# Normalised rows and third parts on GpSimd in the distance stage of a hybrid layer

## The reference, cut to what matters

```python
xn = layernorm(x)                               # per row, eps 1e-5
qh, kh, vh = heads(xn @ Wq), heads(xn @ Wk), heads(xn @ Wv)   # 16 heads of 8
dist = max(q_norm - 2 * qk + k_norm^T, 0)       # q_norm, k_norm: squared lengths
scores = exp(-gamma * 8 ** -0.5 * dist), kept where key > query, else 0
x = x + heads_joined(scores @ vh) @ Wo
```

## Time and profile before

| what | value |
|---|---|
| time, median of 3 runs | 1817.73 us (1814.71 to 1819.59) |
| the profiled execution | 1817.88 us, its span 1816.1 us |
| mean granted TensorE clock | 0.977 |
| busy: PE, DVE, ACT, POOL | 1658.8, 1452.3, 1451.6, 753.4 us |
| distance stage | about the first 456 us of the span |
| later stages | the rest |

### The profile page before, as it was taken

The page is one execution under the profiler, slowest core; times in us unless marked ns, Lnnn a source line. Parts: engine busy times, 40 slices in busy tenths (PEclk is TensorE's granted clock), DMA queues, the critical chain, the costliest instruction groups (busy, mean ns, idle before and its releaser), DMA issues. The chain is left out here.

```text
span 1816.1 us, 68034 instructions
## 1 busy us (share of the span) xinstructions
PE 1658.8 (91%) x27513; PEld 1267.0 (70%) x27513; DVE 1452.3 (80%) x3466; ACT 1451.6 (80%) x4102; POOL 753.4 (41%) x849
## 2 busy tenths in 40 slices
PE   3888899888899999999997987879999999999897
PEld 1444444444688888888886864658888888888686
DVE  8999999998877777877896866747777777789664
ACT  4999999997788988888774657668888888877464
POOL 2010000001255545454546856435555555454694
PEclk7999999999999999999999998989999999999998
DMA  6656555552001010101012000000000010101211
GB/s 188 150 149 159 151 126 154 135 140 41 14 15 26 14 26 14 26 15 26 14 26 49 2 1 1 1 13 22 18 18 23 17 24 16 25 14 26 49 48 48
DMA packets 80040, 91.95 MB, mean 51 GB/s; under 512 B 11696, under 2 KB 67984, under 8 KB 79728
## 3 DMA queue, kind: packets, MB, share of 16 engines
q1 hardware_dynamic: 78432, 87.15, 19.0%
q10 hardware_dynamic: 1296, 0.44, 0.1%
HBM read 39.68 MB, written 31.10 MB: 39 GB/s over the span
## 5 line engine op out<-in xcount | busy, mean ns | idle before, releaser
L1633 POOL TENSOR_TENSOR f1l_pn<-f1l_p,f1l_rs 128x512 f32<-128x512 f32 (+1 forms) x256 | 206.5, 828 | 253.1 <-DVE f1l_rs L1326 248.1
L1633 POOL TENSOR_TENSOR f2l_pn<-f2l_p,f2l_rs 128x512 f32<-128x512 f32 (+1 forms) x256 | 206.4, 828 | 233.9 <-DVE f2l_rs L1326 233.9
L1205 ACT ACTIVATE f2l_p<-f2l_sm,f2l_nb 128x192 f32<-128x192 f32 x512 | 209.6, 435 | 43.0 <-DVE f2l_nb L1319 43.0
L1205 ACT ACTIVATE f1l_p<-f1l_sm,f1l_nb 128x192 f32<-128x192 f32 x512 | 209.8, 435 | 42.4 <-DVE f1l_nb L1319 39.1
L595 ACT ACTIVATE r_pr<-r_far 128x1536 f32<-128x1536 f32 x128 | 194.1, 1517 | 0.7 <-PE r_far L416 0.6
L432 PE MATMUL r_acc<-r_pr,r_vp 128*32 128x384 f32 x3528 | 188.8, 330 | 2.0 <-DVE r_pr L709 0.9
L698 DVE SCALAR_TENSOR_TENSOR r_pr<-r_pr,k_lo,r_cap 128x512 f32<-128x512 f32 x256 | 182.9, 755 | 9.6 <-ACT r_pr L595 9.2
L709 DVE TENSOR_SCALAR r_pr<-r_pr,k_hi,k_lo 128x768 f32<-128x768 f32 x256 | 162.4, 675 | 0.6 <-ACT r_pr L595 0.6
L595 ACT ACTIVATE r_pr<-r_near 128x1024 f32<-128x1024 f32 x128 | 138.4, 1081 | 3.0 <-PE r_near L403 2.9
L1319 DVE TENSOR_REDUCE f2l_nb<-f2l_sm 128x4 f32<-128x768 f32 x128 | 116.1, 948 | 17.1 <-PE f2l_sm L1019 17.0
L1319 DVE TENSOR_REDUCE f1l_nb<-f1l_sm 128x4 f32<-128x768 f32 x128 | 116.1, 948 | 8.6 <-PE f1l_sm L1019 8.6
(11 more groups left out here) (536 smaller groups left out, 5087.9 us busy)
## 6 DMA issues: line engine op xcount, KB each, us to landing
rbf_rows<-r_part SPq DMA_DIRECT2D x112, 128.0 KB, 2.2
r_qs<-rbf_rows SPq DMA_DIRECT2D x60, 192.0 KB
r_ks<-rbf_rows SPq DMA_DIRECT2D x60, 192.0 KB
f1l_vs<-f1l_vv SPq DMA_DIRECT2D x64, 128.0 KB, 2.4
f2l_vs<-f2l_vv SPq DMA_DIRECT2D x64, 128.0 KB, 2.5
rbf_rows<-r_part SPq DMA_DIRECT2D x16, 384.0 KB, 3.1
rbf_rows<-r_part SPq DMA_DIRECT2D x16, 256.0 KB, 3.2
out<-k_x SPq DMA_DIRECT2D x8, 512.0 KB, 3.2
```

Source lines behind the costliest of these rows:

```text
L1205: ins = nc.scalar.activation(p[:, u % 2, k, :], sm[:, u % 2, k // 2, k % 2 * PW:(k % 2 + 1) * PW], ACT.Exp, bias=nb[:, u % 2, k:k + 1], ac ...
L1633: ins = nc.gpsimd.tensor_tensor(pn[:, u % 2, at:at + HU * w].rearrange("p (k c) -> p k c", k=HU), p[:, u % 2, :, cols], r.broadcast_to([P, ...
```

## The change

ScalarE's `norm` and the third parts in VectorE's loop are taken out. GpSimd gets both. Its `norm(b)` makes a whole batch of `z` in two operations of 512 columns: `x` times `rstd`, spread over each row, then, after a wait on the new semaphore `s_zr`, plus `nbias`, spread the same way. Its `third_part` is VectorE's, with the same wait and the same semaphore. GpSimd's list becomes one loop over the batches 2 to 15: the normalised rows, the split of a third of the weights in batches 3 to 5, and the three third parts; the third part of the norms of batch 1 stands behind the rows of batch 2. The third parts of batch 0 and of the queries and keys of batch 1 stay on VectorE (`second_rest`), as do the rows of batches 0 and 1. The copy of the values out of PSUM into `vp` stays on ScalarE (L562). ScalarE's wait for `s_nb` moves to GpSimd.

```diff
@@ -216,6 +216,7 @@
         s_xa = sem("xa")
         s_bn = sem("bn")
         s_nv = sem("nv")
+        s_zr = sem("zr")
         s_nb = sem("nb")
         USES = 5
         PAIRS = RH // 2
@@ -228,7 +229,6 @@
         AFFINE = 16 * len(K["affine"])
         WHOLE = AFFINE + 16 * 3
         TURNED = 2 * B
-        NORM_AT = 4
         FRESH_AT = 3
         SPLIT_AT, THIRD = 1, H * DH
         RUN = B - 3
@@ -533,14 +533,6 @@
                 act.wait_ge(*left_by(b, k))
                 nc.scalar.activation(p[:, 1, :], left, ACT.Copy).then_inc(s_p2, 1)
 
-            def norm(b):
-                wait(act, s_mp, USES * (b - 1) + 1)
-                for j in range(NT):
-                    t = b * NT + j
-                    ins = nc.scalar.activation(z[:, j, :], K["x"][:, t, :], ACT.Identity, scale=rstd[:, t:t + 1],
-                                               bias=nbias[:, t:t + 1])
-                ins.then_inc(s_z, 1)
-
             def leave_values(b):
                 act.wait_ge(s_pv, 4 * (b + 1))
                 wait(act, s_wo, b)
@@ -604,7 +596,6 @@
                 leave(1, k)
             roots(REST, ROOTS)
             nc.scalar.preload_act_table_set("natural_log_exp_and_others")
-            act.wait_ge(s_nb, 1)
             for b in range(B):
                 for w in range(PAIRS):
                     n = PAIRS * b + w
@@ -617,8 +608,6 @@
                         second_part(*split(b, w))
                     if ahead(b, w):
                         leave(*ahead(b, w))
-                    if w == NORM_AT and b < B - 2:
-                        norm(b + 2)
                     if (b, w) == ROOT_AT:
                         roots_next()
                     if (b, w) in ROWS_AT:
@@ -739,8 +728,6 @@
                     n = PAIRS * b + w
                     masked(n)
                     bounded(n)
-                    if split(b, w):
-                        third_part(*split(b, w))
                     if ahead(b, w):
                         remainder(*ahead(b, w))
                     if w == OUT_AT and b:
@@ -762,12 +749,35 @@
             nc.gpsimd.tensor_tensor(cap[:], K["later_key"][:].unsqueeze(1).broadcast_to([P, RH, P]),
                                     K["hi"][:].unsqueeze(2).broadcast_to([P, RH, P]), ALU.mult).then_inc(s_cap, 1)
 
-            for q in range(3):
+            def norm(b):
+                pool.wait_ge(s_mp, USES * (b - 1) + 1)
+                t = slice(NT * b, NT * (b + 1))
+                spread = lambda v: v[:, t].unsqueeze(2).broadcast_to([P, NT, P])
+                nc.gpsimd.tensor_tensor(z[:], K["x"][:, t, :], spread(rstd), ALU.mult).then_inc(s_zr, 1)
+                pool.wait_ge(s_zr, b - 1)
+                nc.gpsimd.tensor_tensor(z[:], z[:], spread(nbias), ALU.add).then_inc(s_z, 1)
+
+            def third_part(b, k):
+                p, left = parts(b, k)
+                pool.wait_ge(s_p2, 3 * b + k)
+                nc.gpsimd.tensor_tensor(p[:, 2, :], left, p[:, 1, :], ALU.subtract).then_inc(s_p3, 1)
+
+            def split_weights(q):
                 w = slice(THIRD * q, THIRD * (q + 1))
                 pool.wait_ge(s_wl, AFFINE + 16 * (q + 1))
                 nc.gpsimd.tensor_copy(K["wqkv_h"][:, w], whole[:]).then_inc(s_wh, 1)
                 pool.wait_ge(s_wh, 2 * q + 1)
                 nc.gpsimd.tensor_tensor(K["wqkv_l"][:, w], whole[:], K["wqkv_h"][:, w], ALU.subtract).then_inc(s_wh, 1)
+
+            pool.wait_ge(s_nb, 1)
+            for b in range(2, B):
+                norm(b)
+                if b == 2:
+                    third_part(1, 3)
+                if 0 <= b - 3 < 3:
+                    split_weights(b - 3)
+                for k in range(1, 4):
+                    third_part(b, k)
 
             pool.wait_ge(s_bn, 4)
             nc.gpsimd.tensor_scalar(nv[:], K["mv"][:, 0:2 * NT, 1], 1.0 + 1e-5, 1e-10, ALU.mult, ALU.add).then_inc(s_nv, 1)
```

## The result

The changed kernel takes 1850.83 us (median of 4 runs, 1846.48 to 1854.61), the kernel before beside it 1816.88 us (4 runs). The ratio is 1.0183, 95% interval 1.017 to 1.0197: 34 us slower, where 1848 us and a range of 1823 to 1866 had been forecast. The profiled execution took 1854.61 us, its span is 1852.5 us, so it is the longest of the four and its rows show 36 us of loss. The next stage's first scale begins at 489.4 us in place of 456.6: 32.8 us are lost in the distance stage.

What follows compares the result with a forecast made beforehand. VectorE and ScalarE were taken as tied limits of the distance stage. 1817.9 us + 59.5 stops - 21.75 third parts - 3.4 gaps - 1.6 first norm - 3 PSUM readers gave 1847.6, said as 1848; range 1823 to 1866.

Steps and rivals of the forecast that it cites:

- What bounds the kernel, and that ScalarE's relief is worth nothing by itself: Distance stage: VectorE (25.16 us) and ScalarE (24.89) tied in a 25.40 us batch; ScalarE's 21.7 us saved credited nothing.
- What is removed from VectorE: The third parts in the distance stage: 21.75 us together, 1.53 us in a full batch.
- The stop as the deciding term: GpSimd's instructions stop VectorE's masking, bounding and third parts: 59.5 us over the stage, 4.2 in a full batch.
- the twin: A later stage's 512-column GpSimd subtraction of two full tensors, taken as a third part's length: 1.27 us.
- VectorE's gaps vanish, -3.4: VectorE's gaps of 0.24 us in 14 batches vanish once it alone is the limit: 3.4 us less.
- the costlier rival: VectorE stands for every GpSimd instruction, or late remainders hold TensorE's next projection: +49 us, 1867; chance 0.11.
- The stops that fall on PSUM readers, -3: Stops falling on VectorE's remainders and residual cost nothing: 3 us less, half of a tenth of the stops.
- Hidden stops: Faster rival: GpSimd's turns fall in VectorE's PSUM readers, statistics or gaps; 21.7 us less, 1796; chance 0.09.
- Cheap stops: Rival: norm operations stop VectorE 0.30 us, third parts 0.8 and 0.3; +8.5 us, 1826; chance 0.15.
- The whole instruction: The costlier rival: VectorE stands for every GpSimd instruction from end to end; +49 us, 1867; chance 0.11.
- third parts late for the loads: Alternative if the batch were long with VectorE idle: diagonals would wait for a DMA; no size or chance given.

Runs made afterwards that it cites:

- `norm_aligned`: Against the kernel before, only the rows move to GpSimd, started when pair 4 is bounded; third parts stay on VectorE: 1818.75 us, ratio 1.0012.
- `third_only`: Against the changed kernel, the rows go back to ScalarE and the third parts stay on GpSimd: 1824.43 us, ratio 1.0029 to the kernel before.
- `dummy`: The kernel before, nothing removed; GpSimd also runs the change's five instructions a batch into scratch tiles whose results no engine uses: 1863.11 us, ratio 1.0241.
- `aligned`: The changed kernel with GpSimd's rows and query and key third parts started to run beside VectorE's remainders, residual and statistics: 1821.15 us, ratio 1.0022.
- `filler`: The changed kernel with four unused identity multiplications on TensorE in pair 3, ahead of its wait for VectorE: 1843.12 us, ratio 1.0121 to the kernel before.

## Why the prediction was right, step by step

- *What bounds the kernel, and that ScalarE's relief is worth nothing by itself*: right. `norm_aligned` takes the rows off ScalarE nearly for free, and the time stays.
- *What is removed from VectorE*, 1.53 us a batch: right; with it and its stops `third_only` closes to 0.12 us (25.16 - 1.53 + 2.13 = 25.76, measured 25.64).
- *The stop as the deciding term*: right in kind, shown by `dummy`; mis-sized by a sixth. A third part of 512 columns stops 0.86 us, not 1.05; one of 256 columns 0.42, not 0.53; a norm operation 0.72, not 0.79. That is 3.6 us a batch in place of 4.2, or 50 us in place of 59.5 by the same counts, and 50.8 by the groups of the stage. Part of it is that the twin was too long: a third part that meets nothing when it starts takes 1.16 us (`aligned`), not the 1.27 of the earlier trace rows. For the rest, no run here tells why.
- *VectorE's gaps vanish, -3.4*: wrong. They grew by 5.7 in 13 batches. The step that failed is "ScalarE at 23.9 and TensorE at 22.7 no longer near it": TensorE's 22.7 holds at full clock only, and in ten of 13 batches it did not have that: the stops make the values wait in pair 3, and there the clock falls in most batches. I had put the knock-on by TensorE into the costlier rival, by way of the remainders and the next projection; it came by way of the values instead, and by the clock. `filler` shows that share as 9 us. A batch of before at a clock of 0.94 and 27.00 us was there to give the price; the prediction makes no use of it.
- *The stops that fall on PSUM readers, -3*: the third parts and rows met masking and bounding in the batches of the timelines; there was little of this.
- The two errors nearly cancel: about 9 us less stop, about 9 us more gap; the 3 us credited for PSUM readers are about what 1848 lacks to 1850.83. So the closeness is in part luck, and the range is what the argument had earned.
- *The rivals.* Hidden stops: out; where I placed the instructions beside PSUM readers on purpose, the loss went from 34 to 4 us, so the mechanism exists, but the change's starting points do not meet it. Cheap stops: out, although the stop lies between the two cases. The whole instruction: out, the stops being 3.6 us a batch where the instructions, met by nothing, would take 1.16 + 1.16 + 0.67 + 1.04 + 1.04 = 5.1. That third parts late for the loads make the loss: out by `third_only`.

## What to carry to other kernels

An idle engine is not free help if its instructions stop the one that is full. Price a move to GpSimd by the stops that its instructions cause on VectorE, read from a place where the two already overlap, and set that against what VectorE loses; a relief of another engine that is tied with VectorE counts for nothing. If it must be GpSimd, start it where VectorE reads PSUM or computes statistics, and do not string such instructions together, since a run of stops may cost TensorE its clock as well. In a wait of TensorE that cannot be removed, multiplications without a use can be cheaper than none, as `filler` shows for this one.

## What I had not expected of the hardware

- TensorE's clock fell behind a wait of 1.17 us that followed lighter work (3.68 us busy of 5): the mean granted clock was 0.52 of full in the next 5 us, and 24 multiplications took 2.79 us instead of 1.50. It did so in nine of the 12 batches with that wait, and in one of the 14 of before, without it. Four multiplications put in the wait kept it at 1.00 in all 13 batches.
- A GpSimd instruction that only writes stops VectorE's bounding (one input, 768 columns in 0.59 us) as a reading one does, 1.05 us beside a memset of 1.50, and leaves its operations with two inputs alone: 0.69 and 1.40 us, as without it. A memset that comes while bounding runs waits itself, 2.12 us in place of 1.50.
- The stop is shorter than the instruction that causes it, by 0.25 to 0.32 us for those of the change: 0.42 of 0.67, 0.86 of 1.16, and 0.72 of the 1.04 that a row operation takes where it meets nothing.
